# Issuing attention's row-maximum passes ahead of their block, in twos and then singly

## The reference, cut to what matters

```python
q = x @ Wq + bq;  k = x @ Wk + bk;  v = x @ Wv + bv
scores = jnp.einsum('bqd,bkd->bqk', q, k) / jnp.sqrt(128.0)
scores = jnp.where(causal, scores, -jnp.inf)
weights = jax.nn.softmax(scores, axis=-1)
out = jnp.einsum('bqk,bkd->bqd', weights, v)
return out @ Wo + bo
```

## Time and profile before

| | before |
|---|---|
| profiled execution, us | 1522.29 |
| its span, us | 1520.5 |
| PE busy, us (share of the span) | 1463.3 (96%) |
| DVE busy | 1008.0 (66%) |
| ACT busy | 734.4 (48%) |
| POOL busy | 344.0 (23%) |
| mean granted clock of PE, as a share of 2.4 GHz | 0.989 |

### The profile page before, as it was taken

How to read it: one execution, slowest core, us unless ns; L and a number is a source line. 1 busy time by engine, 2 the same in 40 slices (tenths; PEclk the granted TensorE clock), 3 DMA queues, 4 the chain that set the end, 5 groups by cost and what they waited for, 6 DMA issues and landing times.

```text
span 1520.5 us, 23833 instructions
## 1 busy us (share of the span) xinstructions
PE 1463.3 (96%) x9472; PEld 1004.2 (66%) x9472; DVE 1008.0 (66%) x1966; ACT 734.4 (48%) x1039; POOL 344.0 (23%) x259
## 2 busy tenths in 40 slices
PE   8999999999999999899999999989999999999998
PEld 6677777777777776444554555546656666677886
DVE  3355555464646467888778778874888888566665
ACT  4333333333333335777877876853434444432333
POOL 0021211120211123000000000001657676750001
PEclk9999999999999999999999999999999999999999
DMA  7203031212130251001100100013100000000112
GB/s 269 81 27 109 28 110 33 104 55 89 49 108 1 87 188 42 14 1 56 56 28 28 56 29 27 1 42 114 37 1 1 1 0 1 0 1 28 56 56 83
DMA packets 43905, 79.93 MB, mean 53 GB/s; under 512 B 7074, under 2 KB 14882, under 8 KB 42387
## 3 DMA queue, kind: packets, MB, share of 16 engines
q1 hardware_dynamic: 43794, 78.41, 15.3%
HBM read 53.24 MB, written 25.17 MB: 52 GB/s over the span
## 4 chain that ended last, share of the span: by engine, by line
PE 63%; issue 19%; DVE 13%; ACT 3%; POOL 1%; DMA 0%; SPq 0%; DVEq 0%; POOLq 0%; ACTq 0%
PE psum L125 13%; PE psum L127 12%; PE psum L126 12%; PE psum L1360 6%; PE psum L1003 3%; PE psum L1010 3%; PE psum L616 2%; DVE sm L464 2%; PE psum L1338 2%; PE psum L642 2%; PE psum L631 2%; PE psum L637 2%; DVE c_mx L1281 1%; PE psum L651 1%; PE psum L646 1%
## 5 line engine op out<-in xcount | busy, mean ns | idle before, releaser
L1003 PE MATMUL psum<-early,high 128*128 128x512 fp8e4 x1024 | 235.0, 382 | 7.9 <-DVE low_r L975 4.2
L1003 PEld LDWEIGHTS psum<-early,high 128*128 128x128 fp8e4 x1024 | 98.2, 98 | 127.7 <-ACT early L880 6.6
L1209 POOL TENSOR_TENSOR c_ls<-c_ls,c_pr 128x512 f32<-128x512 f32 (+2 forms) x136 | 161.9, 1190 | 65.5 <-ACT c_pr L1254 56.3
L410 POOL TENSOR_TENSOR rms<-ms,mhalf 128x16 f32<-128x16 f32 x30 | 87.8, 2926 | 341.9 <-DVE ms L473 341.9
L1254 ACT ACTIVATE c_pr<-c_sc 128x512 f32<-128x512 f32 (+2 forms) x144 | 85.1, 593 | 152.7 <-DVE c_sc L1296 137.7
L1360 PE MATMUL psum<-c_pr,V 128*128 128x512 f32 (+2 forms) x288 | 138.1, 565 | 3.7 <-ACT c_pr L1254 2.5
L125 PE MATMUL psum<-Qh_r,Kh 128*128 128x512 f32 (+1 forms) x272 | 139.7, 513 | 0.0
L1010 PE MATMUL psum<-high,b_act 128*128 128x512 fp8e4 x512 | 118.9, 387 | 2.4 <-DVE Ql_r L980 2.2
L1296 DVE TENSOR_TENSOR c_sc<-psum,c_mb 128x512 f32<-128x512 f32 (+2 forms) x144 | 91.8, 640 | 42.8 <-PE psum L127 32.7
L125 PE MATMUL psum<-early_r,high_r 128*128 128x512 f32 x256 | 106.6, 417 | 5.4 <-DVE early_r L436 5.4
L127 PE MATMUL psum<-Qh_r,Kl 128*128 128x512 f32 (+1 forms) x272 | 105.2, 387 | 0.0
(11 more groups left out here) (238 smaller groups left out, 3245.8 us busy)
## 6 DMA issues: line engine op xcount, KB each, us to landing
low<-x_dram SPq DMA_DIRECT2D x9, 1024.0 KB, 5.5
wst<-in_L_ffn_w_gating SPq DMA_DIRECT2D x16, 512.0 KB, 4.5
xs<-in_L_attn_x SPq DMA_DIRECT2D x8, 1024.0 KB, 7.3
xt<-in_x_turned SPq DMA_DIRECT2D x7, 1024.0 KB, 5.0
x_dram<-xs SPq DMA_DIRECT2D x7, 1024.0 KB, 4.8
x_dram<-low SPq DMA_DIRECT2D x5, 1024.0 KB, 4.3
wst<-in_L_ffn_w_linear SPq DMA_DIRECT2D x16, 256.0 KB, 4.5
high<-x_dram SPq DMA_DIRECT2D x4, 1024.0 KB, 6.6
```

Of the source, the lines that this page charges most:

```text
L410: nc.gpsimd.tensor_tensor(rms_of(b, c), ms_of(b, c), const["mhalf"][:, 0:H], ALU.pow).then_inc(*done)
L1003: last = t.matmul(out[:, h, :], w8g[:, tile + k, (2 * m + h) * P:(2 * m + h + 1) * P], x8[:, u, k, :], start=k == 0, stop=k == DC - 1)
L1209: nc.gpsimd.tensor_tensor(ls[:, i % 2, q0:], ls[:, i % 2, q0:], pr[:, g % SLOTS, q0:], ALU.add).then_inc(*L.done(*name))
```

## The change

It does three things. The eight passes of block 1 leave block 0 and go, with those of block 0, into the end of stage B, one or two at a time between its jobs (`mb 0` and `bias 0` with them). The passes of blocks 2 to 7, 132 in number, make one list that is issued from the first tile of block 0 on: at each tile, as many as the tightest of six due times asks for (the passes of block i+1 by two tiles before the end of block i), rounded up. By that formula it issues 2 at each of the first 22 tiles (all of blocks 0 and 1, tiles 0 to 9 of block 2), 1 at each of the next 88 (to tile 25 of block 6), and none behind them. And the passes of blocks 0 and 1 use banks 4 and 5 by the parity of q + k. No instruction is added or dropped; 18 passes leave blocks 3 to 6 (104 before, 86 after), 10 more lie in blocks 1 and 2 (28 before, 38 after), 8 in both cases in block 0, 8 more in the end of stage B.

```diff
--- before.py
+++ after.py
@@ -1082,18 +1082,26 @@
 
 
 
-    order = max_jobs(0) + [("mb", 0), ("bias", 0)]
+    order = max_jobs(0) + max_jobs(1)[:2] + [("mb", 0)] + max_jobs(1)[2:4] + [("bias", 0)] + max_jobs(1)[4:]
+    ahead = [job for i in range(2, NB) for job in max_jobs(i)]
+    due, n = [], -2
+    for i in range(1, NB - 1):
+        n += tiles(i)
+        due.append((n + tiles(0), sum(len(max_jobs(j)) for j in range(2, i + 2))))
+    n_ahead = len(ahead)
+    g = 0
     for i in range(NB):
-        ahead = max_jobs(i + 1) if i + 1 < NB else []
         tail = [("L", i - 1)] + [("y", i - 1, c) for c in range(CH)] if i else []
         order += [("s", i, k) for k in range(AHEAD)]
         n = tiles(i)
         for k in range(n):
             if k + AHEAD < n:
                 order.append(("s", i, k + AHEAD))
-            take = -(-len(ahead) // max(1, n - 2 - k)) if ahead else 0
+            gone = n_ahead - len(ahead)
+            take = max([-(-(jobs - gone) // (end - g)) for end, jobs in due if end > g and jobs > gone], default=0)
             order += ahead[:take]
             ahead = ahead[take:]
+            g += 1
             if k == n - 1 and i + 1 < NB:
                 order.append(("mb", i + 1))
             order.append(("pv", i, k))
@@ -1101,6 +1109,7 @@
             if tail and (k == 1 or k >= 3):
                 order.append(tail.pop(0))
         order += tail
+    assert not ahead
     order += [("L", NB - 1)] + [("y", NB - 1, c) for c in range(CH)]
 
 
@@ -1159,8 +1168,10 @@
             w = 5 + i % 2
         elif kind == "bias":
             w = 5
-        elif i == 0 and kind in ("mx", "mb"):
-            w = 4 + (name[2] % 2 if kind == "mx" else 0)
+        elif i == 0 and kind == "mb":
+            w = 4
+        elif i <= 1 and kind == "mx":
+            w = 4 + (name[2] + name[3]) % 2
         elif name == ("L", NB - 1):
             w = 4
         elif kind == "y" and i == NB - 1:
@@ -1793,9 +1804,17 @@
         plan += [("B", ("g", 0, 1))] + part("A", ("oT", last, 1), ("r", last, 3)) + [("B", ("u", 0, 1)), ("B", ("g", 0, 2)), ("A", ("oT", last, 2))]
         plan += [("B", ("u", 0, 2)), ("A", ("y", last, 2)), ("B", ("g", 0, 3)), ("B", ("u", 0, 3)), ("A", ("oT", last, 3)), ("B", ("g", 0, 4)), ("A", ("y", last, 3))]
         plan += part("B", ("g", 0, 4), ("u", last, 5)) + [("C", ("ahead", "dve", 0))] + part("B", ("u", last, 5), ("x2", last - 1, 1))
-        plan += part("B", ("x2", last - 1, 1), ("y", last, 1)) + part("C", None, ("mx", 0, CH - 1, 0)) + part("B", ("y", last, 1), ("y", last, CH - 1))
-        plan += [("C", ("ahead", "dve", 1))] + part("C", ("mx", 0, CH - 1, 0), ("mb", 0)) + part("B", ("y", last, CH - 1), ("VT", last - 1)) + part("C", ("mb", 0), ("bias", 0))
-        plan += part("B", ("VT", last - 1), ("VT", last)) + part("C", ("bias", 0), ("s", 0, 1)) + part("B", ("VT", last), None)
+        plan += part("B", ("x2", last - 1, 1), ("y", last, 0)) + part("C", None, ("mx", 0, 1, 0))
+        plan += part("B", ("y", last, 0), ("y", last, 1)) + part("C", ("mx", 0, 1, 0), ("mx", 0, 3, 0))
+        plan += part("B", ("y", last, 1), ("y", last, 2)) + part("C", ("mx", 0, 3, 0), ("mx", 1, 0, 1)) + [("C", ("ahead", "dve", 1))]
+        plan += part("B", ("y", last, 2), ("y", last, 3)) + part("C", ("mx", 1, 0, 1), ("mb", 0))
+        plan += part("B", ("y", last, 3), ("K", last - 1)) + part("C", ("mb", 0), ("mx", 1, 1, 0))
+        plan += part("B", ("K", last - 1), ("Q", last - 1)) + part("C", ("mx", 1, 1, 0), ("mx", 1, 1, 1))
+        plan += part("B", ("Q", last - 1), ("VT", last - 1)) + part("C", ("mx", 1, 1, 1), ("mx", 1, 2, 0))
+        plan += part("B", ("VT", last - 1), ("K", last)) + part("C", ("mx", 1, 2, 0), ("mx", 1, 2, 1))
+        plan += part("B", ("K", last), ("V", last - 1)) + part("C", ("mx", 1, 2, 1), ("mx", 1, 3, 0))
+        plan += part("B", ("V", last - 1), ("Q", last)) + part("C", ("mx", 1, 3, 0), ("mx", 1, 3, 1))
+        plan += part("B", ("Q", last), ("VT", last)) + part("C", ("mx", 1, 3, 1), ("s", 0, 1)) + part("B", ("VT", last), None)
         plan += [("D", ("ahead", "pool", 0))]
         opening = {("pv", last, 14 + n): job for n, job in [(k, ("x", 0, k)) for k in range(DC)] + [(5, ("h", 0)), (7, ("hN", 0)), (15, ("hT", 0))]}
         opening.update({("pv", last, 22 + n): ("gate", 0, n) for n in range(6)})
```

## The result

The changed kernel takes 1512.71 us (median of 5, 1511.65 to 1513.48) against 1520.16 (median of 5, 1518.12 to 1522.81) for the kernel before: ratio 0.9949, 95% interval 0.9934 to 0.9963. It is faster by 7.5 us; 17.6 were forecast. The profiled execution took 1513.40 us with a span of 1511.7. The profiled execution of before lies 2.1 us above its median, so the profiles differ by more (8.9 us) than the medians.

A forecast was written before the change was run, and what follows sets the result against it. PE, busy 96% of the span, was taken as the bound. End of B -1.8, block 0 -2.0, block 1 +0.8, block 2 -0.8, blocks 3 to 6 -13.8: -17.6 us, 1504.7 profiled, median 1502.5, range 1496.5 to 1511.

The forecast's parts named there:

- The end of B: End of stage B: stall, clock, added passes and later Q 7 sum to -1.8 us, between +1 and -3.
- block 0: First block of stage C: two passes per tile instead of four, 9.4 us becomes 7.4, so -2.0.
- The stall: End of stage B: PE's 2.44 us stand at four passes behind y 7 1 goes, -2.4 us.
- the wait before Q 7: End of stage B: PE waits some 1.5 us before Q 7, which starts some 0.8 us later.
- The term of -1.5 for the clock: End of stage B: without the idle the clock no longer falls, -1.5 us; 0 if it falls all the same.
- I take the 9.6, which is also 4 x 2.4: Blocks 3 to 6: passes' bank waits, 9.6 us, put down to DVE's 2.4 us lag per block; -7.6 expected.
- The bounds, 7 to 16 for these blocks: Blocks 3 to 6: forecast gain of 13.8 us, between 7 and 16.
- 0.5 us each for what still catches it idle: Blocks 1 and 2: DVE is the bound with 0.5 us idle each: 21.5 and 28.2 us, +0.8 and -0.8.
- rival 2: Blocks 1 and 2: DVE idles as much as before, +6 us, 1508.5; mark: over 53 us together; chance 0.12.
- Rival 1: Blocks 3 to 6: one pass and a y still bind DVE, 3.2 us less gain, 1506; chance 0.12.
- Rival 3: Blocks 0 to 2: repeated clock falls, about 1.5 us each, 1521 or more; chance 0.05 with other undoing causes.

The follow-up runs named there:

- e2: The kernel before, with POOL's addition of residual and bias cut to 8 columns (output not the reference's): 1512.09 us, ratio 0.9949.
- e3: The changed kernel with only its end-of-stage-B part: later passes at the rate of before, none in block 0: 1513.84 us, ratio 0.9958.
- e6: The kernel with only the end-of-B part of the change, plus POOL's addition early in four parts: 1508.82 us, ratio 0.9926.
- e12: The kernel before, with POOL's addition early in four parts, all work done: 1515.71 us, ratio 0.9964.
- e5: The changed kernel with POOL's addition early, in four parts behind the block's own last four row sums, all work done: 1505.66 us, ratio 0.9895.
- e1: The changed kernel with POOL's addition of residual and bias cut to 8 columns (output not the reference's): 1503.24 us, ratio 0.9891.
- e7: The changed kernel with the early addition in four parts, and from block 3 on y jobs behind tiles 3, 5, 7, 9: 1507.78 us, ratio 0.9918.

## Why the prediction was wrong

**The end of B and block 0 were right in mechanism, and the end of B's size by luck.** The stall went, and the wait before Q 7 was 1.36 us (forecast 1.5). But the measured -1.8 up to the first exponential is made of two parts. From the start of y 7 1 on, the part that the change touches, it is -2.9. The other +1.1 lies ahead of it: y 7 0 starts 1.0 us later in the profile of after, although nothing differs before it (and from y 7 0 to y 7 1 it is 6.0 us in both).

The term of -1.5 for the clock was a matter of chance. The clock never fell there once the idle was gone (twelve kernels of twelve), but with the idle it fell in two of four. The same holds for the other two idles of this size. Ahead of y 7 0 PE stands for 2.2 us in all sixteen profiles, and the clock falls there in twelve; ahead of `mb 3` it stands for 1.80 us in five (before, e2, e3, e6, e12), and the clock falls in two (before, e3). "TensorE: Matmul & The Clock Gate" of the Trainium skill, section "HAM oscillation — how this bites in real kernels", describes falls behind longer waits, for DMA; the prediction drew from it the doubt that an idle so short is not what is followed by a fall. The traces say that a fall can follow such an idle and need not. How often the clock falls also moves the start of stage C: the first exponential comes at 1051.5 to 1052.7 us in the four profiles with no fall at y 7 0, and at 1053.6 to 1056.7 in the others.

**The step that failed is "I take the 9.6, which is also 4 x 2.4".** All of the passes' wait for banks in blocks 3 to 6 was put down to two passes beside a y, on the strength of a sum that happened to fit, and 7.6 us of it were forecast to go. e2 shows that half of it (9.6 to 5.0) comes from POOL's addition with no pass moved, and in the changed kernel the wait only changes its name, from the passes to the first matmuls of the y jobs: 10.4 us. After taking off the 4.1 us of moved work, 3.3 us came back in these blocks, where 9.7 were forecast. Two things were overlooked: that y 0 waits for the addition, and that in block 6 a subtraction on DVE lasts as long as the addition beside it. The change even made the second worse, from 2.52 to 3.28 us. Blocks 3 to 6 by rate and by the addition's place:

| blocks 3 to 6, us | rate of before | even rate |
|---|---|---|
| addition behind L | 182.9 | 175.5 |
| addition early (e12, e5) | 177.4 | 168.9 |
| addition cut down (e2, e1) | 177.2 | 168.7 |

I forecast 169 for the upper right cell; that is what the cells below it hold. The even rate brings 7.4 (8.4 with the addition early), of which 4.1 is work moved to other blocks; the addition brings 6 to 7 more in the changed kernel, about 5 of them by y 0's wait in blocks 3 to 5 and 1.6 to 1.8 by the subtraction in block 6. The upper left cell is alone in having the lower clock and the long subtraction in block 3 (1.73 us instead of 0.61), so the differences from it are somewhat too large as a measure of rate or addition. The bounds, 7 to 16 for these blocks, did hold the 7.4; the value taken was near the wrong end. These blocks are 6.4 us of the shortfall.

**The second step that failed is "0.5 us each for what still catches it idle"** in blocks 1 and 2. DVE's busy time was about right (20.86 and 26.97 against 21.0 and 27.7 forecast), its idle was not: 3.0 and 2.1 us. In block 1 it is 0.96 before `ol`, which waits for ACT; 0.45 before y 0; 1.03 at the block's edge; the rest small gaps. None is POOL's alone: e1 takes only 0.4 us off each block. This is rival 2, whose mark (over 53 us for the two) was only reached: 53.0. The two blocks are 3.3 us of the shortfall.

**The rivals.** Rival 1 (y tiles stay the bound) looked right by its mark, a wait above 4 us, but for another reason: e5 has the same y tiles (2.8 us from y to y on DVE) and no matmul of PE waits for DVE in them; e7, which spreads them, takes only 0.4 us less in blocks 3 to 6. Rival 3 did not come: the clock is 1.00 in all four stretches after. The falls from cycling through banks that the same page of the Trainium skill describes, section "A second HAM failure mode: psum-queue depth-cycling", are not seen in these blocks. With 6.4 us missing in blocks 3 to 6 and 3.3 in blocks 1 and 2, the time lay 1.7 us outside the range.

What stays open: why the clock falls behind one idle of two us and not behind the same one in another execution; why y 7 0, with nothing changed before it, starts anywhere from 1011.3 to 1012.7 us; and what the early addition costs in block 7.

## What to carry to other kernels

Before a wait is priced, look at every engine that the waiting instruction needs: if the engine named in a row had ended well before, another one is the releaser, and "issue" of 0.65 us in the chain of waits says the same. Ahead of evening out one producer's rate, ask what else a consumer that works in order waits for: here a 4.58 us addition on the least busy engine set the pace, and putting it where its engine was free gained 7.0 us on the changed kernel and 4.5 on the kernel before. Look also for an instruction that takes several times its usual length, and at what the other engines run beside it: its row shows no wait. Extra work for a late engine belongs well before or well behind its crowded stretch, not right behind it.

## What the runs showed of the hardware

The same addition in four parts of 128x512 (1.27 to 1.29 us each) costs POOL 5.1 us instead of 4.58.

POOL's addition held up one kind of DVE instruction by being run. A 128x512 subtraction of two tiles that took 0.68 us away from POOL's work took 2.52 us beside the 4.58 us addition in the kernel before and 3.28 in the changed one, and in both ended 0.55 us behind the addition. POOL's row sums did the same on a smaller scale: 1.47 us in e1. The `sub` of the scores, which reads a PSUM bank and one tile, took its usual 0.68 us beside the same addition.

The granted clock fell to its lower level behind PE idles of about two us in some executions and not in others: 12 of 16 behind 2.2 us, 2 of 4 behind 2.4 us, 2 of 5 behind 1.8 us.
